# GpSimd memsets behind every fourth indirect DMA of a graph attention and expert kernel

## The reference

```python
h = (x @ W).reshape(N, H, C)                       # x is layer-normed first
e = leaky_relu(a_src[src] + a_dst[dst], 0.2)
alpha = exp(e - segment_max(e, dst)[dst]) / (segment_sum(...)[dst] + 1e-16)
out = segment_sum(h[src] * alpha[:, :, None], dst).mean(axis=1) + bias
...
for e in range(NUM_EXPERTS):                       # tokens are layer-normed again
    out = out + combine[:, e:e + 1] * (gelu(tokens @ w1[e] + b1[e]) @ w2[e] + b2[e])
```

## Time and profile before

| | us |
|---|---|
| median of 3 runs | 972.01 (971.95 to 973.24) |
| the profiled execution, first to last instruction | 1111.2 |
| TensorE matmul busy, whole span | 718.4 |
| VectorE busy | 659.9 |
| GpSimd busy | 615.4 |
| GpSimd's 392 gathers (L774), busy | 375.7 |

### The profile page before, as it was taken

The page is one execution under the profiler, slowest core; times in us unless marked ns, Lnnn a source line. Parts: engine busy times, 40 slices in busy tenths (PEclk is TensorE's granted clock), DMA queues, the critical chain, the costliest instruction groups (busy, mean ns, idle before and its releaser), DMA issues.

```text
span 1111.2 us, 16087 instructions
## 1 busy us (share of the span) xinstructions
PE 718.4 (65%) x3704; PEld 640.2 (58%) x3705; DVE 659.9 (59%) x1859; ACT 389.4 (35%) x884; POOL 615.4 (55%) x680
## 2 busy tenths in 40 slices
PE   5783330026474566455565366769999998669995
PEld 4782320025364456455565365768888887558985
DVE  6682470554456456454556665875687878654663
ACT  6521011016463444332312111101354423547763
POOL 6666767706656666566666665001614422476686
PEclk9999555558776777787786677888999999789998
DMA  9633054417676666565554544333999785357763
GB/s 338 201 87 77 4 144 110 113 45 229 203 232 192 199 216 196 155 191 166 168 161 135 154 130 131 117 147 128 395 331 342 279 313 174 110 136 118 120 100 41
DMA packets 97019, 189.64 MB, mean 171 GB/s; under 512 B 22975, under 2 KB 55090, under 8 KB 96092
## 3 DMA queue, kind: packets, MB, share of 16 engines
q0 software_dynamic: 31680, 70.52, 26.3%
q1 hardware_dynamic: 50704, 76.07, 20.2%
q10 hardware_dynamic: 14544, 42.02, 9.7%
HBM read 124.75 MB, written 64.74 MB: 171 GB/s over the span
## 4 chain that ended last, share of the span: by engine, by line
PE 33%; DVE 27%; issue 14%; another core or an unknown queue 13%; DMA 6%; ACT 3%; ACTq 1%; DVEq 1%; POOLq 1%; POOL 0%; SPq 0%; PEld 0%; PEldq 0%
PE banks L1161 13%; PE banks L1035 12%; DMA out<-ring 4%; PE banks L1201 3%; PE banks L1214 2%; DVE banks L1440 2%; DVE arena L1835 1%; PE banks L952 1%; PE banks L966 1%; DMA ring<-in_x 1%; ACT arena L1303 1%; ACT banks L1307 1%; DVE arena L1765 1%; ACTq L1289 1%
## 5 line engine op out<-in xcount | busy, mean ns | idle before, releaser
L774 POOL DMA_INDIRECT ring<-node_table,idx x392 | 375.7, 958 | 217.8 <-issue 110.8
L1035 PE MATMUL banks<-arena,ring 128*128 128x160 f32 x1568 | 298.7, 356 | 114.6 <-ACT banks L1309 51.6
L1035 PEld LDWEIGHTS banks<-arena,ring 128*128 128x128 f32 x1568 | 277.5, 234 | 135.5 <-issue 134.7
L1303 ACT COPY arena<-banks 128x400 f32<-128x400 f32 x200 | 88.5, 494 | 389.5 <-PE banks L1035 133.2
L1161 PE MATMUL banks<-ring 128*128 128x264 f32 x544 | 123.1, 386 | 0.0
L1161 PEld LDWEIGHTS banks<-ring 128*128 128x128 f32 x544 | 103.0, 190 | 17.4
L1835 DVE TENSOR_TENSOR arena<-hot,banks 128x640 f32<-128x640 f32 x84 | 65.0, 817 | 79.2 <-PE banks L1035 39.4
L887 POOL DMA_INDIRECT out<-ring x56 | 89.4, 1596 | 32.3 <-DVE ring L2129 12.3
L1201 PE MATMUL banks<-ring 128*128 128x128 f32 x448 | 65.0, 291 | 16.1 <-issue 14.7
L1201 PEld LDWEIGHTS banks<-ring 128*128 128x128 f32 x448 | 60.9, 203 | 24.6 <-issue 17.6
L1214 PE MATMUL banks<-arena,ring 128*128 x224 | 61.8, 400 | 6.4 <-ACT ring L1357 5.8
(11 more groups left out here) (437 smaller groups left out, 1153.5 us busy)
## 6 DMA issues: line engine op xcount, KB each, us to landing
agg_table<-arena ACTq DMA_DIRECT2D x100, 400.0 KB
ring<-agg_table SPq DMA_DIRECT2D x25, 1600.0 KB
ring<-slot_table SPq DMA_DIRECT2D x56, 130.0 KB
ring<-node_table,idx POOLq DMA_INDIRECT x392
ring<-in_x SPq DMA_DIRECT2D x8, 640.0 KB, 10.9
ring<-in_L_gnn_W SPq DMA_DIRECT2D x4, 1024.0 KB, 7.4
arena<-in_L_ffn_w SPq DMA_DIRECT2D x16, 256.0 KB
node_table<-ring SPq DMA_DIRECT2D x5, 640.0 KB
```

The costliest lines, as they stand in the source:

```text
L774: pool.indirect_dma_start(rows[:, slot_of(b), :], None, node_table, bass.IndirectOffsetOnAxis(idx[:, b:b + 1], 0)).then_inc(got[got_of(g)] ...
L1035: m = pe.matmul(columns[:, k, bass.ds(at * (UNIT * H), SPREAD * H)], lhs[:, k * P:(k + 1) * P], weights, start=False, stop=True, skip_grou ...
L1303: act.copy(stage[j][:, k * SLOTS * H:(k + 1) * SLOTS * H], views[k]).then_inc(drained, 1)
```

## The change

GpSimd's stream gets a helper `pause(times)`: for each time, it waits until all earlier increments of `pool_chain` are in, and writes zeros to all of `job_i` with a memset that raises `pool_chain` by one. Nobody reads what is written. The helper is called with four times behind every fourth look-up (L766), every fourth gather (L774) and every fourth scatter (L827). Nothing else is touched.

```diff
+            def pause(times=1):
+
+                for _ in range(times):
+                    pool.wait_ge(pool_chain, count[0])
+                    count[0] += 1
+                    pool.memset(job_i[:, :], 0).then_inc(pool_chain, 1)
+
...
                     pool.indirect_dma_start(node_block[:, t, :], None, block_rows,
                                             bass.IndirectOffsetOnAxis(block_of_i[:, t:t + 1], 0)).then_inc(node_block_in, 16)
+                    if t % QUAD == QUAD - 1:
+                        pause(QUAD)
...
                     pool.indirect_dma_start(rows[:, slot_of(b), :], None, node_table,
                                             bass.IndirectOffsetOnAxis(idx[:, b:b + 1], 0)).then_inc(got[got_of(g)], 16)
+                    if s % QUAD == QUAD - 1:
+                        pause(QUAD)
...
                 pool.indirect_dma_start(starts_table, bass.IndirectOffsetOnAxis(starts_at[:, t:t + 1], 0),
                                         score_all[:, t, H:2 * H], None).then_inc(starts_sent, 16)
+                if t % QUAD == QUAD - 1:
+                    pause(QUAD)
```

## The result

The changed kernel takes 1050.48 us (median of 4 runs, 1048.96 to 1051.83), the kernel before beside it 971.98 (971.71 to 973.24): a ratio of 1.080, with a 95% interval of 1.079 to 1.082. That is 78.5 us slower, where 83 were forecast. The recorded execution, which is the first of these four (1051.83 us), is in line with the forecast too: it ends after 1050.1 us, 61 us sooner than the 1111.2 us of the recording of before. But the reason that was given for those 1111 us is wrong, as the experiments show. They also show that the sign of the change depends on the chip.

The account below looks back on a forecast made before the run. GpSimd's instruction stream was taken to bound the timed runs, the profile's hold-up being due to recording. 104 pauses × 0.80 us = 83 us on top of 972 gave 1055 us, with a range of 990 to 1090.

Parts of the forecast that it names:

- GpSimd's stream sets the end of the timed runs: Without the profiler, GpSimd's sequence of look-ups, gathers and scatters is the bound from 59.42 us on.
- The sum of 971 us from the rows: Whole kernel before, nothing held up: last gather ends at 582.7 us, then landing about 2, last group 43.5, projection and experts 343.1.
- The hold-up belongs to the recorded execution: Late increments beside GpSimd's long DMA runs come mostly from recording, explaining the 139 us between profile and timed runs.
- Starvation is real: Rival: held increments also occur unrecorded and pauses let them through; 923 us if both executions shrink alike; chance 0.13.
- The hold-up is gone from the new profile because 5.8 us is slower than 4 × 1.40: Four gathers and a pause outlast four held increments of 1.40 us, so the new profile's span comes near 1055 us.
- A pause at 0.80 us: Each pause on GpSimd: four memsets of 0.15, three links of 0.06 and 0.03 sum to 0.81 us; 0.80 used.
- the lower bound of 0.60: Smallest pause price in us, if the last memset hides in the 0.30 us before the next DMA; total 62 us.
- L766 behind a CAST: Look-up on GpSimd, taken to show that the gather after a pause's last memset keeps its own gap of 0.28 to 0.30 us.
- Look-ups hidden in 6.9 us of idle: Six look-up pauses, 4.8 us, before the first gather are covered by GpSimd's 6.9 us wait for VectorE.
- 104 × 0.80 = 83: Pauses on the path, 8 at first gathers, 6 at scatters, 90 at other gathers, at 0.80 us each: 83 us.

Follow-up runs that it names:

- pause_1: The changed kernel with one memset in each pause where it has four: 974.56 us, ratio 1.002 to the kernel before (972.75 us).
- before_again: The kernel before, unchanged, recorded a second time: that execution took 1119.83 us, span 1118.1; the kernel's time on that chip was 1115.32 us.
- pause_waited: The changed kernel with one write per pause and a wait for its end before the next DMA: 1113.86 us, ratio 0.998 to the kernel before (1115.32 us).

## Why the prediction came out right, and where it was wrong

- **GpSimd's stream sets the end of the timed runs: right on the chip where they were timed.** Six kernels there follow GpSimd's rhythm, from one write to eight. The sum of 971 us from the rows was nearly right for a free chip. Against pause_1's trace (span 972.4) it had the first gather 5 us late (59.42, 54.5 there) and the end from L1161 on 8 us long (343.1, and 972.4 − 637.7 = 334.7 there), both from a held chip; and it had 10 us too little from the first to the last gather (522, 532.0 there) and 4.5 too little from the last one to its scores (1.25 + 2, 594.3 − 586.5 = 7.8 there). That these nearly cancel is luck. No trace of the kernel before on a free chip exists; the one with a single write, 2 us slower, stands in for it.
- **The hold-up belongs to the recorded execution: wrong.** This is the step that failed, and with it the use made of NOTIFIC — the notification-queue block of the Trainium skill (section 7.1). Recordings on a free chip show no hold-up (972.4 us for pause_1), and on a held chip all 21 runs of the kernel before took 1107 to 1124 us; what differs by 139 us are the chips. What holds increments up on those chips, and whether the writing of records has a part in it there, is open. The 139 us between a profile and the median were read as "recording against running", when they were "one chip against another". The observation that increments arrive late was right, and so was where: front and groups.
- **"Starvation is real" was given 0.13, and it is real on held chips.** The rival's place was right and its size not: 2% there and not 5%. The first scores come 29 to 36 us sooner, but the groups take 19 us longer.
- **The hold-up is gone from the new profile because 5.8 us is slower than 4 × 1.40: wrong in its reason.** It was gone because that execution ran on a free chip. On a held one the same kernel has a span of 1100.8.
- **A pause at 0.80 us: too much.** The writes were sized rightly (154 ns for 150, four in 0.76), but the 0.30 us before the next DMA don't come on top. 0.61 to 0.62 is right, near the lower bound of 0.60. My choice rested on L766 behind a CAST, with its gap of 0.28; but L766 waits for that CAST, and a gather waits for no memset.
- **Look-ups hidden in 6.9 us of idle: wrong on the free chip.** The first gather starts at 54.5 us with one write and at 58.8 with four: 4.3 us on the path. The idle time that should have covered them is not there.
- **Borders: missing.** Six times 1.3 = 8 us (the first border and the last, at blocks 48 and 368, cost nothing over the pause), made of register loads that used to run beside earlier gathers.
- **Together.** The recorded spans of the change and of pause_1 are 77.7 us apart. The first gather has 4.3 of them (58.8 against 54.5), and 73.9 lie between the first gather and the last (605.9 against 532.0): 90 pauses within the groups 57.3 (0.64 each; most add 0.59, some more), the break of the scatters with its pauses 4.9 (39.99 against 35.11), the six borders with their pauses 11.5, and 0.2 for the rest. The forecast had 104 × 0.80 = 83. At the right price these would have been 104 × 0.61 = 64, so 19 us too much in one term and 15 us of terms left out (the borders 8 of them) came out at 83 against 78.5. That the time was met better than its parts is luck.

## What to carry to other kernels

When a profile and the timed runs beside it disagree by over 10%, have both taken once more on one chip before the gap is explained; a verdict on a change near such an effect should be taken on both kinds of chip. The recorded execution may itself be one of the timed ones, and then their agreement shows nothing. On GpSimd between two indirect DMAs, one short instruction that nobody waits for is nearly free; a wait for its end takes away the lead that hides the stream's register loads. And a pause meant to let other engines through must be judged where they are: here, on a held chip, it gained 29 to 36 us in the front, and the groups took 19 longer.

## What was unexpected of the hardware

- The same kernel takes 972 us on one chip and 1115 on two others, with the same instructions, a GpSimd that issues its gathers 1.25 us apart on both (median), VectorE busy for 658 to 660 us in before, before_again and pause_1, and a granted clock that can be the same (0.812 and 0.810) in a trace of 1111 us and one of 972.
- On a held chip VectorE's and TensorE's waits outlast what they wait for while GpSimd issues indirect DMAs: VectorE went on 1.77 us after the end of a run of eight gathers and 3.24 us after the end of TensorE's last weight load. A pause of 0.76 us every fourth DMA ended the long wait of L1493, one of 0.38 did not. From the scores of the last group on, where GpSimd's DMAs are fewer, the held chip is behind by 8 us only. Why some chips hold increments up was not found.
- Traces of held chips hold less than half of the records of semaphore updates that those of free chips hold (7,124 in before, 16,557 in pause_1), though the instructions and DMA packets are all there.
- Independent memsets of 128x50 on GpSimd last 0.15 us and start 0.07 to 0.08 us apart; linked ones start 0.20 to 0.22 us apart.

A version better than both kernels was not found on a free chip: there the kernel before is the fastest that ran. On a held chip the pauses in the front alone might keep the 29 to 36 us without the 19. That is an estimate from the rows above, and pause_waited speaks against it; it was not tried there.
